# Gate and up products of 15 feed-forward steps as seven half-size products, with the contexts kept in memory meanwhile

## The reference

```
h = layernorm(x)
gate, up = h @ Wgate, h @ Wup          # 512 x 1376 each, dequantised: scale * (nibble - zero)
x = x + (silu(gate) * up) @ Wdown      # 1376 x 512
```

## Time and profile before

| | us |
|---|---|
| median of 3 runs | 2426.17 |
| lowest, highest | 2425.99, 2426.36 |
| the profiled execution | 2425.11 |
| its span (first to last instruction) | 2423.3 |
| TensorE busy in the span | 2367.6 (98%) |
| VectorE (DVE) busy | 1625.1 (67%) |
| ScalarE (ACT) busy | 1254.1 (52%) |
| GpSimd (POOL) busy | 1227.8 (51%) |

### The profile page before, as it was taken

The page is one execution under the profiler, slowest core; times in us unless marked ns, Lnnn a source line. Parts: engine busy times, 40 slices in busy tenths (PEclk is TensorE's granted clock), DMA queues, the critical chain, the costliest instruction groups (busy, mean ns, idle before and its releaser), DMA issues.

```text
span 2423.3 us, 45113 instructions
## 1 busy us (share of the span) xinstructions
PE 2367.6 (98%) x17668; PEld 1295.6 (53%) x17668; DVE 1625.1 (67%) x3133; ACT 1254.1 (52%) x2423; POOL 1227.8 (51%) x983
## 2 busy tenths in 40 slices
PE   8899999999999999999999999999999999999998
PEld 4455555555555555444444655555555555555554
DVE  7977777777777798754444666667666666656566
ACT  7666555656555545433232554555555555544443
POOL 4656566666666666233232445445555555445531
PEclk9999999999999999999999999999999999999999
DMA  6111121212121111011101011122121212221101
GB/s 211 45 45 36 44 53 27 53 27 53 32 53 31 42 40 28 27 44 36 44 11 29 27 31 28 44 53 62 36 62 36 62 36 62 53 43 27 27 14 70
DMA packets 216753, 108.13 MB, mean 45 GB/s; under 512 B 169280, under 2 KB 192480, under 8 KB 216544
## 3 DMA queue, kind: packets, MB, share of 16 engines
q1 hardware_dynamic: 216544, 105.25, 17.5%
HBM read 61.62 MB, written 4.19 MB: 27 GB/s over the span
## 4 chain that ended last, share of the span: by engine, by line
PE 65%; POOL 13%; DVE 11%; issue 5%; ACT 5%; DMA 0%; POOLq 0%; DVEq 0%; SPq 0%; ACTq 0%
PE PB L865 18%; PE PB L817 16%; PE PB L977 9%; PE PB L801 6%; PE PB L994 5%; POOL AR L2711 5%; POOL AR L2716 3%; POOL PSP L2729 2%; PE PB L907 2%; PE PB L842 2%; DVE AR L2128 2%; DVE WB L1933 2%; PE PB L773 2%; POOL AR L2706 1%; ACT JUNK L1330 1%
## 5 line engine op out<-in xcount | busy, mean ns | idle before, releaser
L865 PE MATMUL PB<-WB,AR 128*128 128x512 f16 x3072 | 685.5, 380 | 3.4 <-DVE XTB L1952 1.6
L817 PE MATMUL PB<-XTB,WB 128*128 128x512 f16 x3072 | 679.5, 380 | 1.2 <-DVE XTB L1952 0.7
L865 PEld LDWEIGHTS PB<-WB,AR 128*128 128x128 f16 x3072 | 298.3, 98 | 359.0 <-issue 11.1
L817 PEld LDWEIGHTS PB<-XTB,WB 128*128 128x128 f16 x3072 | 297.5, 98 | 345.3 <-issue 5.6
L2722 POOL TENSOR_TENSOR AR<-AR,SML 128x512 f32<-128x512 f32 x128 | 144.6, 1150 | 318.1 <-DVE SML L2113 318.1
L2143 DVE SCALAR_TENSOR_TENSOR X<-PB,SML,X 128x512 f32<-128x512 f32 x256 | 189.5, 747 | 169.4 <-PE PB L865 163.4
L1490 ACT ACTIVATE AR<-PB 128x512 f16<-128x512 f32 x256 | 132.0, 602 | 248.2 <-PE PB L907 248.2
L2023 DVE TENSOR_TENSOR AR<-PB,AR 128x512 f16<-128x512 f32 x128 | 88.2, 690 | 167.9 <-ACT AR L1453 167.9
L2711 POOL TENSOR_TENSOR AR<-AR,CST 128x512 f32<-128x512 f32 x128 | 183.0, 1430 | 33.9 <-ACT AR L1400 33.9
L977 PE MATMUL PB<-XTB,AR 128*128 128x512 f16 (+1 forms) x864 | 192.5, 379 | 0.0
L1994 DVE TENSOR_TENSOR AR<-AR 128x512 f16<-128x512 f32 x128 | 132.9, 1038 | 74.7 <-ACT AR L1406 74.5
(11 more groups left out here) (273 smaller groups left out, 3776.9 us busy)
## 6 DMA issues: line engine op xcount, KB each, us to landing
STG<-in_wo SPq DMA_DIRECT2D x14, 1024.0 KB
STG<-in_wq SPq DMA_DIRECT2D x13, 1024.0 KB
STG<-in_qw_gu SPq DMA_DIRECT2D x40, 128.0 KB
STG<-in_ctxT SPq DMA_DIRECT2D x4, 1024.0 KB
X<-in_x SPq DMA_DIRECT2D x4, 1024.0 KB, 10.3
out_x<-X SPq DMA_DIRECT2D x16, 256.0 KB, 2.4
STG<-in_wk SPq DMA_DIRECT2D x14, 256.0 KB
STG<-in_wv SPq DMA_DIRECT2D x14, 256.0 KB
```

The lines of the kernel that those rows point to most:

```text
L817: m = pe.do.matmul(b[:, :], wq[x][:, k, h * 128:(h + 1) * 128], XT[y][c][:, k, :], start=n == 0, stop=n == 11)
L865: m = pe.do.matmul(b[:, :], AT[x][:, h, t * 128:(t + 1) * 128], wo[y][:, h, :], start=n == 0, stop=n == 11)
```

## The change

Of the 24 steps, 15 are folded: all with s = 1 to 4 but (1, 0). In these the product of a 512 x 256 weight block for gate and for up with 512 x 512 activations is done by Strassen's scheme over halves: the 512 features in two halves ki, the inner tile j, and the tokens in two halves (token tiles 0, 2 and 1, 3). Gate and up lie side by side in one bank of 2 x 256 columns. Seven products P1 to P7, each of 12 matmuls with 256 columns, take the place of eight; sums make the four blocks (j, t).

- **Operands.** Four sums of activation blocks are made once per chunk: `join_x` (POOL, high + low to f32), `fold_x` (POOL, a chain of four subtractions), `fold_x_halves` (ACT high, DVE low). Four sums of weight blocks are made once per step s: `fold_w` (POOL, in the unpacked f32 weights in STG) and `fold_w_halves` (ACT, POOL). The SIDE table gives them places between (0, 2) and (1, 3), and at (2, 2) and (3, 2). The unpacking of step 2 moves two slots later.
- **Results.** P1 and P5 are copied from their banks by ACT into f32 buffers, P6, P2, P7, P3, P4 are added by DVE, and P5 is added to two of them by POOL (`add_p5`). Silu, product, high and low half are then made for each of four blocks with 256 tokens rather than two tiles with 512.
- **Place.** The activation sums lie in CTB. So SP writes the contexts' halves to device memory after unit 12 of layer 0 (four DMAs of 1 MB), and reads each back after product P4 of step (4, c).
- **Waits.** The area of gate and up weights is free for the next load when the weights' halves are done; layer norm of layer 1 and load w(1, 1, 2) wait for the last product of step 4.

```diff
         every = []
+        kept = nc.dram_tensor("kept", (128, 4096 * NC), F16, kind="Internal").ap()
 
         def signal(name):
...
+        FW = AR[:, 11776:13824].bitcast(F16)
+        FW0 = [LNB.rearrange("p a d -> p (a d)").bitcast(F16), STG[:, 3072:4096].bitcast(F16)]
+        SUMW = {1: [[FW[:, 2048 * n + 512 * i:2048 * n + 512 * i + 512] for i in range(4)] for n in range(2)],
+                0: [[FW0[n][:, 512 * i:512 * i + 512] for i in range(4)] for n in range(2)]}
+        SUMX = [[[CTB[:, (2 * c + n) * 2048 + 512 * i:(2 * c + n) * 2048 + 512 * i + 512] for i in range(4)] for c in range(NC)]
+                for n in range(2)]
+        XF = [WB[1][:, 6144 + 1024 * i:7168 + 1024 * i].bitcast(F32) for i in range(4)]
+        CB = [PSP[:, a, :, :].rearrange("p q n -> p (q n)").bitcast(F32) for a in range(2)] + [AR[:, 5120:5632], WB[0][:, 8416:9440].bitcast(F32)]
+        BLOCK = {(0, 0): 0, (1, 0): 1, (1, 1): 2, (0, 1): 3}
+
...
+        def step_tiles(s):
+            return [128, 128] if s < 5 else [96]
+
+        def folded(s, c):
+            return 1 <= s <= 4 and (s, c) != (1, 0)
+
+        def last_gate_up(s):
+            return (s, NC - 1, "P4") if folded(s, NC - 1) else (s, NC - 1, len(step_tiles(s)) - 1, 1)
+
...
@@ -335,7 +376,8 @@
             LOADS += [(("gu", s + 1), (0,)), (("dn", s + 1), (1,))]
             if 1 <= s <= 3:
                 LOADS += [(w(1, 0, s - 1), (6,))]
-        LOADS += [(("l1",), (0,)), (w(1, 1, 1), (1,)), (w(1, 1, 0), (0,)), (w(1, 1, 2), (1,)),
+        LOADS += [(("l1",), (0,)), (("ct", 0), ()), (("ct", 1), ()), (w(1, 1, 1), (1,)), (("ct", 2), ()), (w(1, 1, 0), (0,)),
+                  (("ct", 3), ()), (w(1, 1, 2), (1,)),
                   (w(1, 2, 1), (0,)), (w(1, 2, 0), (1,)), (w(1, 2, 2), (0,))]
         LOADS += [(w(1, g, k), ((g + k) % 2,)) for g in range(3, NKV) for k in range(3)]
         LOADS += [(("tail",), (0, 1))]
@@ -479,12 +521,21 @@
                 plan_f(0, 2, slot, name, 1, 3, half)
         for s in range(5):
             for k in range(KT):
-                where = (((2, 3), (3, 0), (3, 1), (3, 2)), ((0, 3), (1, 1), (1, 3), (2, 1)))[s][k] if s < 2 else \
+                where = (((2, 3), (3, 0), (3, 1), (3, 2)), ((1, 1), (1, 3), (2, 1), (2, 3)))[s][k] if s < 2 else \
                     (k // 2, 1 + 2 * (k % 2))
                 plan_f(s, *where, "unpack", s + 1, k)
                 plan_f(s, *where, "unpack_hi", s + 1, k)
             for j in range(2 if s < 4 else 1):
                 plan_f(*(((0, 3, 3), (1, 0, 1))[j] if s == 0 else (s, 2, 2 + j if s == 1 else 1 + 2 * j)), "unpack_d", s + 1, j)
+
+        for step, first, second in ((1, (0, 3, 3), (1, 0, 0)), (2, (1, 3, 0), (1, 3, 1)), (3, (2, 2, 0), (2, 2, 1)),
+                                    (4, (3, 2, 0), (3, 2, 1))):
+            plan_f(*first, "fold_w", step)
+            plan_f(*second, "fold_w_halves", step)
+        for c, places in ((1, ((0, 2, 1), (0, 2, 3), (0, 3, 1))), (2, ((1, 0, 1), (1, 0, 3), (1, 1, 1))),
+                          (3, ((1, 1, 2), (1, 1, 3), (1, 2, 1))), (0, ((1, 2, 2), (1, 2, 3), (1, 3, 1)))):
+            for name, where in zip(("join_x", "fold_x", "fold_x_halves"), places):
+                plan_f(*where, name, c)
 
...
+            def keep_contexts():
+                for c in range(NC):
+                    sp.wait_ge(c_hi, (("c", c), 3))
+                    sp.wait_ge(c_lo, (("c", c), 3))
+                    sp.do.dma_start(kept[:, 4096 * c:4096 * c + 4096], CTB[:, 4096 * c:4096 * c + 4096]
+                                    ).then_inc(ct_kept[c].of(c, 16), 16)
...
+                    c = key[1]
+                    sp.wait_ge(gu_mm, (4, c, "P4"))
+                    sp.wait_ge(ct_kept[c], c)
+                    sp.do.dma_start(CTB[:, 4096 * c:4096 * c + 4096], kept[:, 4096 * c:4096 * c + 4096]
+                                    ).then_inc(ct_back[c].of(c, 16), 16)
...
+                        sp.wait_ge(gu_mm, last_gate_up(4))
                     if key == w(1, 0, 0):
...
+            def product(s, c, name, b, wt, xs):
+                for g in range(2):
+                    n = 0
+                    o = b[:, 256 * g:256 * g + 256].rearrange("p (a n) -> p a n", a=2)
+                    for k in range(2):
+                        for x, y in THREE:
+                            m = pe.do.matmul(o, wt[x][:, k, g, :], xs[y][:, k, :, :], start=n == 0, stop=n == 5)
+                            n += 1
+                m.then_inc(gu_mm.of((s, c, name)), 1)
+
+            def folded_first(s, c):
+                pl = place(s)
+                for k in range(KT):
+                    pe.wait_ge(uq_hi, (s, k))
+                    pe.wait_ge(uq_lo, (s, k))
+                a11, a12 = [[w_part(GUW[pl][n], ki, 0) for n in range(2)] for ki in range(2)]
+                b11, b21 = [[x_part(n, c, ki, 0) for n in range(2)] for ki in range(2)]
+                sw = [[SUMW[pl][n][i].rearrange("p (k g n) -> p k g n", k=2, g=2) for n in range(2)] for i in range(4)]
+                sx = [[by_kan(SUMX[n][c][i]) for n in range(2)] for i in range(4)]
+                product(s, c, "P1", bank(0, (p_out, (s, c, "P1"))), a11, b11)
+                pe.wait_ge(ws_hi, (s, 3))
+                pe.wait_ge(ws_lo, (s, 3))
+                pe.wait_ge(xs_hi, (c, 3))
+                pe.wait_ge(xs_lo, (c, 3))
+                product(s, c, "P6", bank(1, (p_sum, (s, c, "P1+P6"))), sw[1], sx[1])
+                product(s, c, "P5", bank(2, (p_out, (s, c, "P5"))), sw[0], sx[0])
+                product(s, c, "P2", bank(3, (p_sum, (s, c, 0, 0))), a12, b21)
+
+            def folded_last(s, c):
+                pl = place(s)
+                a22 = [w_part(GUW[pl][n], 1, 1) for n in range(2)]
+                b22 = [x_part(n, c, 1, 1) for n in range(2)]
+                sw = [[SUMW[pl][n][i].rearrange("p (k g n) -> p k g n", k=2, g=2) for n in range(2)] for i in range(4)]
+                sx = [[by_kan(SUMX[n][c][i]) for n in range(2)] for i in range(4)]
+                product(s, c, "P7", bank(1, (p_sum, (s, c, "P1+P6+P7"))), sw[2], sx[2])
+                product(s, c, "P3", bank(2, (p_sum, (s, c, 0, 1))), sw[3], b22)
+                product(s, c, "P4", bank(3, (p_sum, (s, c, 1, 0))), a22, sx[3])
+
...
+            def fold_w_halves(s):
+                for i, (j, ki) in enumerate(((1, 1), (0, 0), (1, 0), (0, 1))):
+                    act.wait_ge(wf, (s, i))
+                    act.do.activation(SUMW[place(s)][0][i].rearrange("p (k g n) -> p k g n", k=2, g=2),
+                                      w_part(AREA[0].rearrange("p (k f) -> p k f", k=4), ki, j), copy
+                                      ).then_inc(ws_hi.of((s, i)), 1)
+
...
+            def product_out(s, c, name, bank, block):
+                before_it = FFN[FFN.index((s, c)) - 1]
+                act.wait_ge(gu_mm, (s, c, name))
+                if folded(*before_it):
+                    act.wait_ge(hf, (*before_it, *block))
+                act.do.activation(CB[BLOCK[block]], PB[bank][:, :], copy).then_inc(p_out.of((s, c, name)), 1)
+
+            def folded_gate(s, c, j, t):
+                act.wait_ge(p_sum2 if (j, t) == (1, 1) else p_sum, (s, c, j, t))
+                for key in h_keys(*FFN[FFN.index((s, c)) - 1], j):
+                    if len(key) == 3 or key[3] == t:
+                        act.wait_ge(h_lo, key)
+                act.do.activation(sg_part(j, t), CB[BLOCK[j, t]][:, 0:256], ACTF.Silu, scale=power(("sc", 0))).then_inc(silu_ok.of((s, c, j, t)), 1)
+
+            def folded_hidden(s, c, j, t):
+                i = FFN.index((s, c))
+                act.wait_ge(hf, (s, c, j, t))
+                act.wait_ge(y_mm, (*FFN[i - 2], 3))
+                act.do.activation(hb_part(s, c, 0, j, t), sg_part(j, t).rearrange("p (a n) -> p a n", a=2), copy
+                                  ).then_inc(h_hi.of((s, c, j, t)), 1)
...
+                if folded(s, c):
+                    product_out(s, c, "P1", 0, (0, 0))
+                    product_out(s, c, "P5", 2, (1, 1))
+                    folded_gate(s, c, 0, 0)
+                    folded_hidden(s, c, 0, 0)
+                    side("f", s, c, 1)
+                    side("f", s, c, 2)
+                    folded_gate(s, c, 1, 1)
+                    folded_gate(s, c, 0, 1)
+                    folded_hidden(s, c, 1, 1)
+                    folded_gate(s, c, 1, 0)
+                    folded_hidden(s, c, 0, 1)
+                    folded_hidden(s, c, 1, 0)
+                    side("f", s, c, 3)
+                    continue
...
+            def fold_x_halves(c):
+                for i in range(4):
+                    dve.wait_ge(xs_hi, (c, i))
+                    dve.do.tensor_tensor(SUMX[1][c][i], XF[i], SUMX[0][c][i], ALU.subtract).then_inc(xs_lo.of((c, i)), 1)
+
+            def product_add(s, c, key, name, bank, dst, src):
+                dve.wait_ge(gu_mm, (s, c, name))
```

(81 more changed lines are left out.)

74 lines of the change are left out of this document (58 added, 16 removed).

## The result

| | before | after |
|---|---|---|
| median us (4 runs each, in one comparison) | 2426.08 | 2473.30 |
| span of the profiled execution | 2423.3 | 2471.4 |

The ratio is 1.0199, 95% interval 1.0187 to 1.0211: 47.2 us slower, 19 us above the end of my range. TensorE did save what it should, so 47.2 + 17.8 = 65.0 us were lost again, where I had counted 32.2.

The account below looks back on a forecast made before the run. The feed-forward was taken as bound by TensorE alone. Profiled 2425.1 - 17.8 saved + 29.0 stall + 3.2 gave 2439.5, beside the median 2440.6, said as 2440 us; range 2412 to 2454 (the forecast's own 2428 to 2452, chance 0.55).

Parts of the forecast that it names:

- TensorE's cadence: In folded steps, 84 matmuls of 256 columns would run at 109.2 ns each, start to start.
- the 17.8 us: TensorE's saving in gate and up products: 1.19 us a step over 15 folded steps.
- the contexts at nothing: Writing the contexts out after unit 12 and reading them back from (4,0) to (5,0) was costed at nothing.
- no loss near unit 13: Transposes of unit 13 would not lose time behind the context transfers; queueing with no cover would cost 12 us, once.
- Taken step by step: From (1,0) to (2,0), following POOL's queue and its waits, TensorE would stall 29.0 us.
- 0.8, 2.9, 10.2 and 15.1: Stalls in us, counted from down to down, before the down products of (1,0), (1,1), (1,2) and (1,3).
- 1.6 each, 3.2 us: At (2,2) and (3,2), POOL's fold_w and halves would bring the last hidden at 22.0 us, where TensorE wants it at 20.4.
- Rival (c): Worse: contention of 5 to 11 us plus 7 us of slower TensorE clock after stalls, 2452 to 2458; 0.15 with (d).
- The contention: DVE and POOL instructions reading SBUF exclude each other: 7 us on DVE, 4 on POOL, 11 at most.
- Floor only (a): POOL's waits overlap with the joins from (1,0) to (2,0), only 12.4 us of stall stay: 2421; chance 0.2.
- all hidden (b): Slack of down product and PSUM banks, or cheaper POOL joins, hides all stalls: 2408.4; chance 0.1.
- (d): 256 columns read in two pieces run at 123 ns, so folded products save nothing: 2458; chance 0.15 with (c).

Follow-up runs that it names:

- x0: Kernel before plus only the contexts' halves written out and read back, with the related waits, no step folded: 2423.8 us, ratio 0.9997.
- x3: Changed kernel without activation sums for chunks 2, 3 and 0 and without weight sums for steps 2 to 4: 2424.5 us, 0.9996 of the kernel before.
- x5: Changed kernel with the second down unpack of step 2 moved from slot (1,2,3) to (1,3,1): 2468.8 us, 1.0182 of the kernel before.
- x6: Changed kernel with ACT's squares of the first layer 1 weights at slot 0 of (s,2) instead of slot 3: 2464.0 us.
- x8: Changed kernel folding twelve steps (s = 2 to 4), unpacks apart, squares early, stages placed where their input is long ready: 2427.2 us.
- x10: x8 with fold_x and fold_w in two halves, activation sums a slot earlier, step 2 down unpacks in (1,3), peak moved: 2428.8 us.
- x12: x10 with the users of banks 4 and 5 (unpack, down unpack, peak) set apart in (1,2) and (1,3): 2432.8 us.
- x1: Changed kernel without the activation sums for chunks 2, 3 and 0, all weight sums kept: 2442.6 us, 1.0075 of the kernel before.
- x9: Changed kernel, 15 folded steps, second step 2 down unpack moved, squares early, weight sums of steps 3 and 4 spread: 2458.7 us.
- x2: Changed kernel without the weight sums for steps 2, 3 and 4, all activation sums kept: 2443.7 us, 1.0079 of the kernel before.
- x4: Changed kernel with join_x of chunks 3 and 0 moved on POOL from slot 2 to slot 3, behind the second add_p5: 2474.6 us.

## Why the prediction was wrong

**Right.** TensorE's cadence and the 17.8 us; step lengths of 15.2, and 14.8 to 14.9 in s = 4 (15.4 in the last); the contexts at nothing (x0); no loss near unit 13, and only a 0.78 us wait in s = 4; the sign, that POOL's one-time work between (1, 0) and (1, 3) and at (2, 2) and (3, 2) is what starts the loss (x3). POOL's prices were good too: `join_x` 4.47 for four (I took 4.8), `fold_x` 5.31 and `fold_w` 5.37 (5.1), the weights' halves 4.67 to 6.27 (4.6), `add_p5` 1.26 (1.27).

**The signs that did not come.** POOL was to be near 9 tenths over (1, 0) to (1, 3) and without idle time at `join_x`: it was busy for 78.0 of 106.0 us, 7 tenths, and idle ahead of `join_x` and of the unpacks. TensorE was to wait in P2 of (1, 2) and (1, 3) and in P6 of (2, 0): it waited at none of the three. And none of its long waits before a down product was for POOL's hidden halves; DVE's down sums (L2453) ended all of them.

**The step that failed: the chain "Taken step by step", of POOL's lag and of where TensorE meets it.** It gave 29.0 us up to (2, 0); it was 45.6 (the first five rows of the table). The down products of (1, 0) to (1, 3) began at 1094.05, 1115.75, 1152.95 and 1177.61. Counted from down to down as the chain does, its parts 0.8, 2.9, 10.2 and 15.1 were 7.6, 6.5, 21.6 and 9.9. Two things in it were wrong.

*POOL's lag was too small.* POOL's rows: its down unpack ahead of `fold_w(1)`, the wait for ACT in (1, 1), the one ahead of `join_x(3)`, the last hidden halves of (1, 1), the down unpack in (1, 2), and the last hidden halves of (1, 2) and (1, 3):

```profile
1071.75 1.16 POOL L2974 TENSOR_TENSOR AR<-STG,AR 128x512 f16<-128x512 f32 x1 [2.47 <-ACT AR L1666]
...
1099.76 1.16 POOL L2967 TENSOR_TENSOR AR<-STG,AR 128x512 f16<-128x512 f32 x1 [1.65 <-ACT AR L1654]
1103.44 4.49 POOL L2990 TENSOR_TENSOR WB<-XTB 128x512 f32<-128x512 f16 x4 [2.52 <-DVE CTB L2418]
...
1112.22 1.30 POOL L3025 TENSOR_TENSOR AR<-AR 128x256 f16<-128x256 f32 x2 [0.81 <-ACT AR L1724]
...
1131.60 1.15 POOL L2974 TENSOR_TENSOR AR<-STG,AR 128x512 f16<-128x512 f32 x1 [5.05 <-ACT AR L1666]
...
1141.45 1.30 POOL L3025 TENSOR_TENSOR AR<-AR 128x256 f16<-128x256 f32 x2 [0.81 <-ACT AR L1724]
...
1175.26 1.31 POOL L3025 TENSOR_TENSOR AR<-AR 128x256 f16<-128x256 f32 x2 [0.81 <-ACT AR L1724]
```

The last hidden halves of (1, 1), (1, 2) and (1, 3) end at 1113.5, 1142.8 and 1176.6, where the chain had 1105.3, 1131.1 and 1161: 8.2, 11.7 and 15.6 us late. Of the 8.2, 4.1 are there when `fold_w(1)` begins (1072.9 for 1068.8), and 4.2 are idle time in (1, 1), for which the chain had next to none: 1.65 us for ACT, and 2.52 because `join_x(3)` writes the same four f32 buffers that DVE's low halves of chunk 2 still read. In (1, 2) the wait for the down unpack was 5.05, not 2.4; in (1, 3) POOL was idle for 9.5 us, not 7.8, and the weights' halves took 6.27, not 4.6.

*TensorE was let wait only at its down products and in P2.* The chain takes the unpacks in its steps as 0.42 us of time. But an unpack on TensorE is also a wait for a bank that DVE must have emptied, and DVE was the engine that stood behind the late `add_p5`. So TensorE stopped there before it came to the down product, with P1, P6 and P5 behind it; after the 13.13 us the down product of (1, 2) began 10.2 us behind POOL's last hidden half. And I took the moved unpacks of step 2 for time alone, without asking what then shares their slot: 5.5 us (x3).

How the 16.6 us above plan divide: the down product of (1, 3) began 1.0 us behind POOL's last hidden half, so at the end of the stretch 15.6 of them are POOL's lag, and the side work is mostly the place where TensorE paid for it. x5 agrees. Without the 13.13 us wait, POOL's last hidden half of (1, 3) came 2.1 us sooner and that down product 1.1 us sooner (counted in both from the 1.3 us wait ahead of (1, 0)). That the buffers of `join_x` and the late start make POOL's lag is read from the trace; no run frees them. The 1.45 us ahead of (1, 0), within the 7.6, come from DVE's low halves of the first chunk, 1.3 us each.

**The same step, in (1, 0).** ACT's halves of the weight sums wait for POOL's chain of four, and the silu of (1, 0) stands behind them. ACT and DVE in the changed kernel:

```profile
1076.86 1.15 ACT L1695 ACTIVATE AR<-STG 128x512 f16<-128x512 f32 x2 [2.06 <-POOL STG L3006]
1078.21 0.63 ACT L1695 ACTIVATE AR<-STG 128x512 f16<-128x512 f32 x1 [0.20 <-POOL STG L3006]
1078.75 0.67 ACT L1678 ACTIVATE AR<-PB,SML 128x512 f32<-128x512 f32 x1
```

```profile
1079.45 0.75 DVE L2412 SCALAR_TENSOR_TENSOR AR<-AR,SML,PB 128x512 f32<-128x512 f32 x1 [8.44 <-ACT AR L1678]
```

The chain follows only POOL's queue here and does not name ACT's halves. A stage that waits in a queue costs every stage behind it.

**"1.6 each, 3.2 us" for (2, 2) and (3, 2)** was 10.4 + 9.2 = 19.6. The lag itself was about right (2.70 and 1.70 us, though at P2); missed was the peak matmul, which waits for ACT's squares, which stand behind the unpack that DVE does after the late hiddens: 4.41 and 5.59 us. x6 moves the squares alone and gets 8 to 9 us back.

**The clock.** Rival (c) had it, as 7 us and "partly under POOL's lag". Its 5 us at half rate, which no row showed then, is what the longest took (1082.85 to 1087.94). On TensorE's timeline it was 13, a fifth of the loss, since there were a dozen waits rather than three. But some 9 of the 13 lie in (1, 0) to (1, 3), where the last down product came 1.0 us behind POOL's last hidden half: there a faster TensorE would mostly have waited longer. How much the clock adds to the run's time is not shown.

**The contention** of rival (c) exists, on both engines. DVE's low halves of the chunk sums (min/median/max ns), four of them while POOL mostly stood idle, and four beside POOL's halves of the weight sums:

```profile
L2418 DVE TENSOR_TENSOR CTB<-WB,CTB x16: 678/1357/1639, 1057.0 to 1164.7; 128x512 f16<-128x512 f32 x16
```

```profile
1100.23 3.04 DVE L2418 TENSOR_TENSOR CTB<-WB,CTB 128x512 f16<-128x512 f32 x4 [1.22 <-ACT CTB L1704]
...
1160.44 5.88 DVE L2418 TENSOR_TENSOR CTB<-WB,CTB 128x512 f16<-128x512 f32 x4 [5.03 <-ACT CTB L1704]
```

```profile
1161.06 6.27 POOL L3012 TENSOR_TENSOR STG<-STG,LNB 128x512 f16<-128x512 f32 x4
```

DVE took nearly twice as long for the same work, and POOL 6.27 us where its halves at 1078.14, with none of these beside them, took 4.67. The 16 of DVE were busy 19.0 us, 8.2 over 16 times the least duration. POOL lost the 1.6, and 0.45 on each of four more instructions that ran beside them, 3.4 in all. I had given 7 and 4. The Trainium skill ("SBUF — State Buffer", Who interferes with whom) has the two exclude each other for a whole instruction; the trace agrees that both are slower side by side, 5.88 for 3.04 and 6.27 for 4.67 us, but shows no instruction that waited for a whole one of the other. POOL's 1.6 us in (1, 3) are part of its lag; how much more of this lies on the path no run separates.

**The rivals.** Floor only (a) and all hidden (b) are out: the sum gave too little, not too much. (c) named the clock, at about half its size on TensorE's timeline, and the contention, and its 2452 to 2458 is too low as well. (d) is out by the cadence. What stays open: which part of the 15.7 to 21.9 us that x8, x10 and x12 lose is contention, which part the longer chain over four engines, and whether an arrangement exists that hides it.

## What to carry over

When a change puts a burst of work on an engine with idle time, ask how far every queue can run ahead, the bottleneck's own included: list each small instruction of the bound engine which waits for a bank or a buffer that a late engine must free, and look for the lag at the first of them, not at the consumer that you have in mind. Follow the late engine's own waits as well: here its lag went beyond the plan more by them than by its work. A stage placed ahead of its input holds all that stands behind it on that engine, so place it where its input is long ready, and leave the slots of shared banks alone. If each named wait that you take away comes back elsewhere, the lag behind it is the likelier cause: then folding less (8 steps of the 15 gained 3.5 us, 15 lost 47) is worth more than another arrangement.

## What the runs showed that I had not expected

- The half-width hidden product on DVE takes 0.48 us with its third input from AR (and 0.48 in the median from PSP), and 0.96 from WB, hardly varying, in the same 15 steps. Nothing in these runs says why.

```profile
L2426 DVE SCALAR_TENSOR_TENSOR AR<-AR,SML x15: 483/485/486, 1109.7 to 1369.4; 128x256 f32<-128x256 f32 x15
L2426 DVE SCALAR_TENSOR_TENSOR AR<-AR,SML,WB x15: 956/961/966, 1110.7 to 1370.4; 128x256 f32<-128x256 f32 x15
```

- POOL adds two f16 inputs to f32 at 1.12 us for 512 elements, faster than f32 with f32 (1.27).
- The length of a wait does not tell whether the clock falls. In the changed kernel the twelve down matmuls behind the 3.36 us wait in (1, 0) took 5.30 us, and the window from 1080 to 1090 stands at 0.66; behind the 3.25 us wait at 1103.99 it is 1.00. Behind the same wait in (1, 0) (3.34 to 3.36 us) they took 2.76 in x1, x3 and x9, 4.08 in x2, 4.32 in x6, and 5.30 in x4 and x5.
